# Last stage of a mixture-of-experts block: the norm moved to ScalarE, the gated product kept in its matmul bank, and stores asked for one place later

## What is computed

```python
shared = jax.nn.silu(xf @ sg) * (xf @ su) @ sd
...
out_e = jnp.einsum('ech,ehd->ecd', h, wd)
gathered = out_e[flat_e, jnp.minimum(pos, capacity - 1)]
contrib = gathered * (flat_g * keep.astype(xf.dtype))[:, None]
routed = jnp.zeros_like(xf).at[tok].add(contrib)
return (shared + routed).reshape(b, s, d)
...
x = _layernorm(x + _L0_ffn_ref(x, ...), axis=-1)
```

## Time and profile before

| | us |
|---|---|
| median of 3 runs (2178.28 to 2179.53) | 2179.31 |
| the profiled execution, its own time | 2181.61 |
| its span, first to last instruction | 2179.8 |
| last stage, from its first DMA request at 1897.2 to the end | 282.6 |
| PE busy in those 282.6 | 240.73 |
| DVE, ACT, POOL busy in them | 208.66, 73.30, 184.20 |
| granted TensorE clock in them | 0.92 of full |

### The profile page before, as it was taken

How to read it: one execution, slowest core, us unless ns; L and a number is a source line. 1 busy time by engine, 2 the same in 40 slices (tenths; PEclk the granted TensorE clock), 3 DMA queues, 4 the chain that set the end, 5 groups by cost and what they waited for, 6 DMA issues and landing times. The chain is left out here.

```text
span 2179.8 us, 51607 instructions
## 1 busy us (share of the span) xinstructions
PE 2008.5 (92%) x14104; PEld 1753.8 (80%) x14104; DVE 1572.4 (72%) x3671; ACT 1228.6 (56%) x3408; POOL 1491.9 (68%) x1707
## 2 busy tenths in 40 slices
PE   5999869999999999976999999999999999387798
PEld 2555548888888788765999999999999999276687
DVE  3666536877878778764777778888888888167976
ACT  3555446666666656632777777777777777132231
POOL 2666521577766777663777778888888888285765
PEclk9999979999999999998999999999999999699899
DMA  4300013233242332403677767777767777244752
GB/s 129 97 0 0 0 43 127 79 123 112 78 155 78 105 127 77 141 25 126 218 233 235 242 218 231 234 235 233 239 231 233 232 232 232 109 181 174 234 172 87
DMA packets 244901, 329.86 MB, mean 151 GB/s; under 512 B 50074, under 2 KB 167234, under 8 KB 244836
## 3 DMA queue, kind: packets, MB, share of 16 engines
q1 hardware_dynamic: 218788, 279.97, 39.7%
q0 software_dynamic: 26048, 49.10, 6.1%
HBM read 236.17 MB, written 77.18 MB: 144 GB/s over the span
## 5 line engine op out<-in xcount | busy, mean ns | idle before, releaser
L1191 POOL DMA_INDIRECT slot_token<-a_entry,a_slot_i x256 | 262.9, 1027 | 113.8 <-issue 71.4
L1687 POOL DMA_INDIRECT part_rows<-e_out,e_dest x184 | 210.9, 1146 | 74.1 <-issue 67.1
L1820 ACT ACTIVATE e_sg<-e_g 128x256 f32<-128x256 f32 x368 | 142.0, 386 | 203.6 <-PE e_g L1512 202.5
L1679 POOL DMA_INDIRECT e_xg<-x_rows,e_tok x188 | 196.6, 1045 | 84.0 <-issue 56.3
L1869 DVE TENSOR_TENSOR e_h<-e_sg,e_u 128x256 f32<-128x256 f32 x368 | 158.0, 429 | 98.6 <-PE e_u L1512 39.6
L1011 ACT ACTIVATE a_prob<-a_s,a_ntop 128x128 f32<-128x128 f32 x512 | 180.9, 398 | 0.6 <-DVE a_ntop L1382 0.5
L1695 POOL TENSOR_TENSOR e_wd1l<-e_raw_d,e_wd1h 128x256 fp32r<-128x256 f32 x184 | 145.4, 823 | 17.2 <-ACT e_wd1h L1800 16.4
L1695 POOL TENSOR_TENSOR e_wd0l<-e_raw_d,e_wd0h 128x256 fp32r<-128x256 f32 x184 | 146.0, 827 | 14.3 <-ACT e_wd0h L1800 13.5
L1884 DVE TENSOR_SCALAR e_out<-e_d,e_dest 128x256 f32<-128x256 f32 x184 | 80.7, 480 | 102.3 <-PE e_d L1512 102.3
L1512 PE MATMUL e_d<-e_wd1h,e_ht1h 128*128 128x256 f32 x368 | 109.3, 297 | 24.6 <-issue 24.6
L866 PE MATMUL a_o<-a_wo,a_ot 128*128 128x256 f32 x512 | 123.5, 385 | 7.9 <-DVE a_ot L1449 7.9
(11 more groups left out here) (330 smaller groups left out, 7537.9 us busy)
## 6 DMA issues: line engine op xcount, KB each, us to landing
e_raw_g<-in_eg SPq DMA_DIRECT2D x94, 512.0 KB
e_raw_u<-in_eu SPq DMA_DIRECT2D x94, 512.0 KB, 5.5
e_raw_d<-in_ed SPq DMA_DIRECT2D x93, 512.0 KB, 5.0
part_rows<-a_zero SPq DMA_DIRECT2D x16, 2048.0 KB, 9.3
f_part<-part_rows SPq DMA_DIRECT2D x16, 2048.0 KB, 10.1
x<-in_x SPq DMA_DIRECT2D x16, 512.0 KB, 3.6
x_rows<-x SPq DMA_DIRECT2D x16, 512.0 KB
out_rows<-f_res SPq DMA_DIRECT2D x16, 512.0 KB, 3.4
```

What stands on the lines that cost most here:

```text
L1191: pool.indirect_dma_start(k.slot_tok, bass.IndirectOffsetOnAxis(ap=slot_i[:, j, q:q + 1], axis=0), entry[:, j, q, :], None, bounds_check=S ...
L1679: pool.indirect_dma_start(xg[a][:, n, :], None, k.x2_d, bass.IndirectOffsetOnAxis(ap=tok[a][:, n, 0:1], axis=0))\
L1687: pool.indirect_dma_start(k.part_d, bass.IndirectOffsetOnAxis(ap=dest[a][:, n, 1:2], axis=0), out[a][:, n, :], None).then_inc(put[a], 16)
L1820: act.activation(sg[m % 2][:], bank_g[m % 2][:, 0:SETW], ACT.Silu).then_inc(sg_rdy, 1)
```

## The change

Three things are done at once, all in `combine_stage`.

1. `normed(q)` moves from DVE to ACT. Where DVE computed (x - mean) x rstd in one operation, ACT computes rstd x x + off, so POOL's `rstd(q)` makes two more small values, `nm` = -mean and `off` = nm x rstd. On ACT the first group of `closing(f)` is normed before `hidden_high(f, 3)`, the second after `turned(f+1)`.
2. The gated product is written over the up product: `hid = bank_u`. DVE's product goes to the bank that it read, and ACT's `hidden_high` and DVE's `hidden_low` read it there. PE may write a `u` bank again only after `hl_rdy` (`hidden_low` of the product two before) instead of `hid_rdy` (its multiplication).
3. `store(q - 4)` becomes `store(q - 5)`, asked for at the same place of the loop.

```diff
-        sg, hid = ([p.sb(f"{n}{i}", [P, GW]) for i in range(2)] for n in ("sg", "hid"))
+        sg = [p.sb(f"sg{i}", [P, GW]) for i in range(2)]
...
+        hid = bank_u
...
+        LAG = RING + 1
...
-                    if q >= 4:
-                        store(q - 4)
-                for q in range(NG - 4, NG):
+                    if q >= LAG:
+                        store(q - LAG)
+                for q in range(NG - LAG, NG):
                     store(q)
...
                     pool.tensor_scalar(ve[a][:], mv[a][:, :, 1], EPS, None, ALU.add).then_inc(rs_rdy, 1)
-                    pool.wait_ge(rs_rdy, ONE + 2 * q + 1)
+                    pool.tensor_scalar(nm[a][:], mv[a][:, :, 0], -1.0, None, ALU.mult).then_inc(rs_rdy, 1)
+                    pool.wait_ge(rs_rdy, ONE + 4 * q + 2)
                     pool.tensor_tensor(rs[a][:], ve[a][:], k.mhalf[:], ALU.pow).then_inc(rs_rdy, 1)
+                    pool.wait_ge(rs_rdy, ONE + 4 * q + 3)
+                    pool.tensor_tensor(off[a][:], nm[a][:], rs[a][:], ALU.mult).then_inc(rs_rdy, 1)
...
-                        for w, bank, used, done in ((wg, bank_g, sg_rdy, g_done), (wu, bank_u, hid_rdy, u_done)):
+                        for w, bank, used, done in ((wg, bank_g, sg_rdy, g_done), (wu, bank_u, hl_rdy, u_done)):
...
+                def normed(q):
+                    a = q % 2
+                    act.wait_ge(rs_rdy, ONE + 4 * (q + 1))
+                    if q not in FULL and q >= RING:
+                        act.wait_ge(stored[q % RING], DMA + 16 * (q // RING))
+                    for j in range(TG):
+                        last = act.activation(res[q % RING][:, j, :], whole(q)[:, j, :], ACT.Identity,
+                                              bias=off[a][:, j:j + 1], scale=rs[a][:, j:j + 1])
+                    last.then_inc(res_rdy, 1)
...
+                    for q in closing(f)[0:1]:
+                        normed(q)
                     hidden_high(f, HC - 1)
                     if f + 1 < NF:
                         turned(f + 1)
+                    for q in closing(f)[1:]:
+                        normed(q)
+                for q in range(FULL[NF - 2], NG):
+                    normed(q)
...
                     if f:
                         summed(f - 1)
-                    for q in closing(f):
-                        normed(q)
                 for q in range(FULL[NF - 2], FULL[NF - 1]):
                     moments(q)
-                    normed(q)
                 summed(NF - 1)
                 moments(NG - 1)
-                normed(NG - 1)
```

More of the change, by code:

```diff
@@ L1915, in combine_stage @@
         xt = [p.sb(f"xt{h}", [P, DC, GW], F32R) for h in "hl"]
-        sg, hid = ([p.sb(f"{n}{i}", [P, GW]) for i in range(2)] for n in ("sg", "hid"))
+        sg = [p.sb(f"sg{i}", [P, GW]) for i in range(2)]
         ht = [[p.sb(f"ht{i}{h}", [P, HC, GW], F32R) for h in "hl"] for i in range(2)]
         stat, mv = ([p.sb(f"{n}{i}", [P, TG, w]) for i in range(2)] for n, w in (("stat", 6), ("mv", 2)))
-        ve, rs = ([p.sb(f"{n}{i}", [P, TG]) for i in range(2)] for n in ("ve", "rs"))
+        ve, nm, rs, off = ([p.sb(f"{n}{i}", [P, TG]) for i in range(2)] for n in ("ve", "nm", "rs", "off"))
         bank_t = [p.bank(f"t{i}") for i in range(2)]
@@ L1958, in opening, with whole @@
             return range(FULL[f], FULL[f + 1] if f + 1 < NF else NG)
+        def whole(q):
+            return (res if q in FULL else acc)[q % RING]
         with nc.Block() as block:
@@ L2086, in _ @@
             def _(act):
-                begin(act, xh_rdy, sg_rdy, hh_rdy)
+                begin(act, xh_rdy, sg_rdy, hh_rdy, res_rdy)
                 def turned(f):
@@ L2113, in _ @@
                         turned(f + 1)
+                    for q in closing(f)[1:]:
+                        normed(q)
+                for q in range(FULL[NF - 2], NG):
+                    normed(q)
             @block.vector
             def _(dve):
-                begin(dve, xl_rdy, hid_rdy, hl_rdy, sum_rdy, mv_rdy, res_rdy)
+                begin(dve, xl_rdy, hid_rdy, hl_rdy, sum_rdy, mv_rdy)
                 def turned(f):
@@ L2139, in summed @@
                                           acc[q % RING][:, 2 * h:2 * h + 2, :], ALU.add).then_inc(sum_rdy, 1)
-                def whole(q):
-                    return (res if q in FULL else acc)[q % RING]
                 def moments(q):
@@ L2151, in moments @@
                     if q >= 2:
-                        dve.wait_ge(rs_rdy, ONE + 2 * (q - 1))
+                        dve.wait_ge(rs_rdy, ONE + 4 * (q - 1))
                     apart(dve, k.past_dve)
@@ L2160, in moments @@
                     last.then_inc(mv_rdy, 1)
[L2162 to L2170, removed]
                 turned(0)
```

## The result

| | before | after |
|---|---|---|
| median of 4 runs, us | 2179.2 (2178.28 to 2179.53) | 2157.84 (2156.66 to 2162.04) |
| span of the profiled execution | 2179.8 | 2155.7 |
| first up matmul of the last stage starts | 1900.92 | 1899.84 |
| from there to the end, the **stage time** | 278.88 | 255.86 |

The ratio is 0.9903, with a 95% interval of 0.9891 to 0.9915: 21.4 us faster, inside the range of 2145 to 2165, 5.5 us above the point forecast and just inside the upper end of the narrower range given for the forecast case, 2146 to 2158. What happened in the stage is better read from the stage time: it fell by 23.0 us, where 27.0 were forecast. The miss to explain is 4.0 us.

A forecast was written before the change was run, and what follows sets the result against it. PE bounds rounds 7 to 12; rounds 1 to 6 lose time to DVE's norm and low halves and to late parts. Round 7 starting 29.9 us earlier, less 2.9, nets 27.0: 2179.3 - 27.0 = 2152.3 us, range 2145 to 2165.

The forecast's parts named there:

- the forecast case: The whole stage goes as the summed steps say: 2152.3 us, own range 2146 to 2158, chance 0.62.
- So 0.48 us a round, 13 rounds: 6.2 us: Up products 2 and 3 of each round: PE waits 0.24 us for bank u behind `hidden_low`, a cost of 6.2 us.
- So I expect no fall, and round 1 at 17.5: Start of round 1: PE's idle time falls below 3 us, so its clock stays up and the round takes 17.5 us.
- A round of 17.5: Length in us of a round that PE bounds, read from round 2 and rounds 7 to 12 of the kernel before.
- The price of the bank edit: DVE's product and `hidden_low`: 0.69 us each unchanged; PE starts round 1 3.36 us earlier; 6.2 us lost to bank u.
- Part 3's cover: Fetch of group 6's parts: landed at 1974.4, wanted by POOL at 1976.9, so 2.5 us to spare.
- The medians: Step from profiled execution to median of runs: the median taken as 2.3 us below that execution's time.
- (a): DVE's product: writing a bank in place is slow; 2161 us at half the bound, 2170 at the bound; chance 0.14.
- (c): Bank u's way back becomes the bound and the kernel slower, 2185 us at 1.5 us each product; chance 0.04.
- (d): Rounds 3 to 6: DVE freed for nothing, as POOL holds bank operations too or DMA paces; about the time before; chance 0.03.
- (b): First rounds stay late: late part or slower POOL, stall of some 6 us at round 5, low clock; 2158 to 2161; chance 0.12.
- (e): Better: DVE's bank write is quicker and the 6.2 us vanish; 2146 us, or 2143.5 with round 5 in time; chance 0.05.

The follow-up runs named there:

- part 3 alone: The kernel before with only the stores asked for one place later, `store(q - 5)`: 2170.73 us, ratio 0.9956.
- part 1 alone: The kernel before with only the product written in the bank and bank u handed back by `hidden_low`: 2182.41 us, ratio 1.0009.
- the kernel with the low half first: The changed kernel with DVE's `hidden_low` of product m-1 moved ahead of the multiplication of product m: 2154.19 us, ratio 0.9887.
- part 1 left out: The changed kernel with the product back in SBUF and bank u handed back after the multiplication: 2163.91 us, ratio 0.9926.
- part 3 left out: The changed kernel with stores asked for at the place they had before: 2162.97 us, ratio 0.9921.

## Why the prediction was right, and where it was short

By its own steps, in stage time, where 27.0 us of gain were forecast and 23.0 came:

- **The bottleneck** was named rightly: norm, low halves and late parts in rounds 1 to 6. Those gave all of the gain, and the kernels with one part left out show each at work.
- **"So 0.48 us a round, 13 rounds: 6.2 us"** is the term that was mis-sized. The mechanism, its two places and the lateness of 0.24 were right. Each costs 0.38, since the weight load itself waits and is uncovered; the prediction put that at nothing. 26 x 0.38 = 9.9 us. That is 3.6 of the miss.
- **"So I expect no fall, and round 1 at 17.5"** failed: 1.7 us, and a low clock in round 1 was one of the prediction's own signs of being wrong. It was drawn from three idle pieces, of 3.63 us and more, and took the one without a fall for a bound. A piece of 2.52 has now gone both ways, and so has one of 3.63 (with part 3 alone the clock fell behind it); this belonged into the sum as a chance, not as nothing. The first matmul behind a piece, which the prediction read, does not show the clock that follows either. With part 1 alone it took 0.50, and the clock fell 1.2 us later:

```profile
1918.36 0.50 PE L1512 MATMUL f_g<-f_xth,wg_h 128*128 128x512 f32 x1 [2.52 <-DVE f_xtl L2123]
```

```profile
1919.70:1922.90 3.20, 3.20 (x9) 2.55 (x8) 0.00 (x0) 0.60 (x1) 3.12 (x2) 0.50 1.02 416
```

- **A round of 17.5** is 17.54 where nothing waits (the kernel with the low half first). Over rounds 1 to 6, which were priced with it: 0.2. The idle piece ahead of round 1 fell by 3.21 instead of 3.36, another 0.2, and round 5 was 0.1 longer than its neighbours.
- **In its favour** came 1.1 in round 0, whose first matmuls ran at the low clock for 5.7 us before and for 3.4 after, though the change does not touch them; 0.5 ahead of round 5, where the stall made round 4 2.1 us longer for 2.6; and 0.2 behind it, from round 7 to the end. The sum: 3.6 + 1.7 + 0.2 + 0.2 + 0.1 - 1.1 - 0.5 - 0.2 = 4.0. The 1.1 is luck: it covers most of the 1.7 that the clock cost in round 1. Why round 0 got its clock back sooner was not tried.
- **The price of the bank edit.** 0.69 for the write in place was right (0.70 here), and the extra time for VectorE's bank reads, which the prediction estimated from the Trainium skill, was not borne out: 684 ns at the median from the bank. What I gave the edit as gain, 3.36 us in round 0, was too narrow a view. Its other effects, shown by the kernel with part 1 left out, are on POOL's additions and on the last `hidden_low` ahead of round 5. The forecast's timeline had them without naming them, as it priced a group of POOL at 9.7 from a stretch of short additions and that `hidden_low` as nothing.
- **Part 3's cover** of 2.5 us was right: with part 3 left out, parts asked for 4.9 us late made POOL wait 2.40. That a fetch would be late without part 3 the prediction had read from SP's queue; I wrongly gave it up in a later expectation.
- **The medians.** The prediction took 2.3 us off, since the profiled execution of the kernel before lay that much over its median. The one after lay 0.4 under its own, and its last stage began 1.1 earlier. That is the rest of the 5.5: 4.0 - 1.1 + 2.3 + 0.4 = 5.6.

Of the rivals, (a), (c) and (d) are ruled out: the write in place is not slow, and no round waits for it once the order is changed. What (b) put together happened in part, through the clock of round 1 and not through a late part. (e) came true only with the order changed.

## What to carry to other kernels

When a buffer's hand-back moves to a later operation, look at what stands ahead of that operation on its engine, and whether the two can be swapped: here the swap removed the 9.9 us of stalls, which no engine's busy time showed. By itself it shortened the stage by 5.7 us, and by 8.6 once the norm stood behind the high halves. Price a short wait of TensorE as its lateness plus the weight load that it leaves uncovered, 0.13 us in all at each of 26 places here. What is gained ahead of a chain on another engine turns into idle time, and the longer idle piece can cost a fall of the clock on top, so mend that chain together with what feeds it.

## What was not expected of the hardware

- In this stage, over all kernels here, none of nine idle pieces of PE from 1.21 to 1.93 us brought the low clock. One of 2.29 did, 2.52 did five times of six, 2.82 both times, 3.63 once of two (it did not in the earlier trace rows), and all fifteen from 4.16 us up did. The low clock began inside the piece or up to 1.3 us behind its end. The length of the idle piece alone does not decide it; what else does was not found.
- VectorE's `hidden_low` with two SBUF inputs slows GpSimd's additions too, from 2400 to 2792 ns on the average of `both`. VectorE's norm, with one tensor and two scalars a partition from SBUF, does not (2392 ns), though it is itself held up by them: 9.49 us for four operations that take 1.37 undisturbed.
